# Second-layer matmuls of a fused attention and FFN block in 64-row halves, two units at a time

## The reference

```python
x = L0_attn_x                                    # 8 x 1024 x 256
q, k, v = split(x @ w_qkv.T + b_qkv)             # 16 heads of 16
q, k = rope(elu(q) + 1), rope(elu(k) + 1)
attn = softmax(q @ k.T / 4) @ v
x = layernorm(x + attn + conv3(v))
h = 2 * relu(s0 * concat(x, -x) @ sign(k0))      # 512 -> 1024
h = 2 * relu(s1 * h @ sign(k1))                  # 1024 -> 1024, the second layer
x = layernorm(x + s2 * h @ sign(k2))             # 1024 -> 256
```

## Time and profile before

| | |
|---|---|
| median of 3 runs | 2095.31 us (2095.06 to 2096.69) |
| profiled execution | 2094.53 us, its span 2092.4 us |
| TensorE busy | 2043.8 us, 98% of the span |
| VectorE busy | 1685.7 us, 81% |
| ScalarE busy | 1489.0 us, 71% |
| GpSimd busy | 1013.3 us, 48% |
| granted TensorE clock | 0.985 of full speed over the span |

### The profile page before, as it was taken

How to read it: one execution, slowest core, us unless ns; L and a number is a source line. 1 busy time by engine, 2 the same in 40 slices (tenths; PEclk the granted TensorE clock), 3 DMA queues, 4 the chain that set the end, 5 groups by cost and what they waited for, 6 DMA issues and landing times.

```text
span 2092.4 us, 43715 instructions
## 1 busy us (share of the span) xinstructions
PE 2043.8 (98%) x17150; PEld 802.9 (38%) x17150; DVE 1685.7 (81%) x3094; ACT 1489.0 (71%) x2867; POOL 1013.3 (48%) x583
## 2 busy tenths in 40 slices
PE   5999999999999999999999999999999999999998
PEld 3132323343433434334343343434343343434355
DVE  8989988788887988888887888878888788888143
ACT  3399888766877678776787767777687766867642
POOL 2968287614757158462585328661475704300010
PEclk7699999999999999999999999999999999999999
DMA  5001210020010200021000200002001010000000
GB/s 199 20 17 47 72 24 31 22 72 13 15 37 31 80 16 16 30 77 42 9 27 27 89 22 17 29 16 99 12 17 37 29 62 17 17 9 29 1 21 21
DMA packets 40429, 76.87 MB, mean 37 GB/s; under 512 B 15024, under 2 KB 19488, under 8 KB 37280
## 3 DMA queue, kind: packets, MB, share of 16 engines
q1 hardware_dynamic: 34496, 49.97, 8.3%
q0 software_dynamic: 5184, 23.07, 3.0%
q10 hardware_dynamic: 544, 1.05, 0.1%
HBM read 46.27 MB, written 25.17 MB: 34 GB/s over the span
## 4 chain that ended last, share of the span: by engine, by line
PE 86%; DVE 8%; ACT 3%; issue 1%; SPq 0%; DMA 0%; POOL 0%; POOLq 0%; ACTq 0%
PE unit_banks L761 27%; PE unit_banks L625 22%; PE o_bank L670 22%; PE unit_banks L697 5%; PE unit_banks L774 5%; DVE maxima L1032 5%; ACT probs L855 2%; PE unit_banks L685 2%; PE unit_banks L635 2%; DVE hT L1101 1%; PE unit_banks L678 1%; ACT rows L943 0%; DMA lepe_rows<-in_b_v 0%; ACT work L897 0%; DVE rows L1161 0%
## 5 line engine op out<-in xcount | busy, mean ns | idle before, releaser
L1032 DVE TENSOR_REDUCE maxima<-unit_banks 128x1 f32<-128x512 f32 x2048 | 1302.5, 682 | 285.4 <-PE unit_banks L625 281.7
L855 ACT ACTIVATE probs<-unit_banks 128x512 f32<-128x512 f32 x2048 | 1115.5, 605 | 491.1 <-PE unit_banks L635 487.6
L625 PE MATMUL unit_banks<-k_stack,q_stack 48*128 48x512 f16 x2048 | 636.5, 388 | 6.2 <-DVE maxima L1032 2.7
L635 PE MATMUL unit_banks<-q_stack,k_stack 50*128 50x512 f16 x2048 | 634.0, 383 | 5.3 <-ACT probs L855 3.2
L670 PE MATMUL o_bank<-probs,v_pair 128*32 128x256 f32 x8192 | 565.3, 387 | 4.0 <-issue 4.0
L761 PE MATMUL unit_banks<-h0T,w 128*128 128x512 f16 x2048 | 480.2, 380 | 0.1
L1439 POOL TENSOR_TENSOR attn<-o_rows_sb,rden 128x256 f32<-128x256 f32 x63 | 39.2, 622 | 743.1 <-DVE rden L1045 739.5
L670 PEld LDWEIGHTS o_bank<-probs,v_pair 128*32 128x32 f32 x8192 | 207.0, 109 | 306.3 <-issue 206.0
L625 PEld LDWEIGHTS unit_banks<-k_stack,q_stack 48*128 48x128 f16 x2048 | 121.8, 94 | 433.2 <-issue 241.3
L761 PEld LDWEIGHTS unit_banks<-h0T,w 128*128 128x128 f16 x2048 | 188.6, 98 | 249.3 <-issue 55.6
L1104 DVE SCALAR_TENSOR_TENSOR h1T<-unit_banks,h1T 128x512 f16<-128x512 f32 x128 | 87.3, 682 | 77.9 <-ACT h1T L919 77.8
(11 more groups left out here) (151 smaller groups left out, 1677.8 us busy)
## 6 DMA issues: line engine op xcount, KB each, us to landing
rows<-in_x POOLq DMA_DIRECT2D x8, 1024.0 KB, 6.3
q_stack<-q_scratch SPq DMA_DIRECT2D x128, 64.0 KB, 2.0
k_stack<-k_scratch SPq DMA_DIRECT2D x128, 64.0 KB, 2.0
work<-in_xT SPq DMA_DIRECT2D x7, 1024.0 KB, 8.1
q_scratch<-parts POOLq DMA_DIRECT2D x14, 512.0 KB, 3.3
k_scratch<-parts POOLq DMA_DIRECT2D x14, 512.0 KB, 3.2
out<-rows SPq DMA_DIRECT2D x7, 1024.0 KB, 4.9
q_stack<-q_scratch SPq DMA_DIRECT2D x128, 32.0 KB, 1.9
```

The source lines that it names most:

```text
L625: nc.tensor.matmul(units.out(unit), q_stack[row:row + STACK, r, t * P:(t + 1) * P], k_stack[row:row + STACK, r, half * 512:(half + 1) * 51 ...
L635: nc.tensor.matmul(units.out(unit), k_stack[row:end, r, kt * P:(kt + 1) * P], q_stack[row:end, r, half * 512:(half + 1) * 512], start=True ...
L855: nc.scalar.activation(probs[:, 2 * (kt % 2) + h, half * 512:(half + 1) * 512], units.out(unit), ACT.Exp, scale=exp_regs[2 * (n % PAIRS) + ...
L1032: nc.vector.reduce_max(maxima[:, v // T % 2, h * T + t, half:half + 1], units.out(unit), AXIS_X)\
```

## The change

Two neighbouring units of the second layer are made together, as a pair (`hidden_pair`). Each hidden tile of 128 rows is split into its upper and lower 64 rows. In the first half of the work (parts 0 and 1) the first unit takes the products over rows 0 to 63 and the second those over rows 64 to 127; in the second half (parts 2 and 3) they cross over. So two matmuls of 64 rows stand side by side at any time, each in its own bank, as S and T do. A pair has four pieces of 16 half matmuls where two units had four pieces of 8 whole ones. In front of part 2 TensorE waits for a new semaphore, that both units' first halves have ended. Both units end with part 3. All units of the second layer are in pairs but the last batch's and the last two units of the batch before it: 220 pieces are changed.

The steps of the pieces in the table are the same for most; the numbers are now written per piece (`deal_at`). A pair takes two banks with part 0 and gives both back after part 3. `Units` counts 0.9 for each of the two units of a piece, where it counted 1.4 for a piece.

```diff
+def in_pair(unit):
+    return unit[0] == "L1" and unit[1] < NB - 1 and not (unit[1:3] == (NB - 2, 1) and unit[3] >= KF - 2)
+
+def units_of(piece):
+    unit = piece[0]
+    return [unit, unit[:3] + (unit[3] + 1,)] if in_pair(unit) else [unit]
...
 def pieces_of(unit):
+    if in_pair(unit):
+        return [(unit, part) for part in range(4)] if unit[3] % 2 == 0 else []
...
         if m < TAIL - 1:
-            deal(b + 26, hidden_units("L1", m, 0, range(1)))
...
-            deal(b + 36, hidden_units("L1", m, 0, range(3, KF)))
+            deal_at(b, (26, 27, 29, 31, 33, *range(35, 46)), hidden_units("L1", m, 0))
             deal(b + 47, hidden_units("L0", m, 1), 2)
             deal(b + 54, out_units(m, 0))
-            deal(b + 58, hidden_units("L1", m, 1, range(6)))
...
+            deal_at(b, (*range(58, 70), 71, 73, 75, 77), hidden_units("L1", m, 1))
...
-DENSE_WRITING = 1.4
+DENSE_WRITING, SHARED_WRITING = 1.4, 0.9
...
+            crossings = [0]
+
+            def hidden_pair(first, second, part):
+                _, m, th, u = first
+                phase, quarter = divmod(part, 2)
+                if part == 0:
+                    units.wait_free(pe, first)
+                    units.wait_free(pe, second)
+                    crossings[0] += 2
+                elif part == 2:
+                    pe.wait_ge(rows_crossed, crossings[0])
+                for k in range(4 * quarter, 4 * quarter + 4):
+                    if u == 0 and phase == 0:
+                        units.wait_read(pe, ("L0", m, th, k))
+                    for i in range(2):
+                        for side in range(2):
+                            unit = second if side != phase else first
+                            r = slice(ROWS * side, ROWS * (side + 1))
+                            done = nc.tensor.matmul(units.out(unit), w1[r, k, unit[3] * P:(unit[3] + 1) * P], h0T[r, i, k, :],
+                                                    start=phase == 0 and k == 0 and i == 0,
+                                                    stop=phase == 1 and k == KF - 1 and i == 1, skip_group_check=True)
+                            if k == KF - 1 and i == 1:
+                                done.then_inc(units.full_sem(unit) if phase == 1 else rows_crossed, 1)
```

More of the change, by code:

```diff
@@ L140, in deal, with deal_at @@
             at[step + i // a_step].append(piece)
+    def deal_at(b, places, units):
+        for place, piece in zip(places, (piece for u in units for piece in pieces_of(u))):
+            at[b + place].append(piece)
     for c in range(1, NB):
@@ L159, in dealt @@
         if m < TAIL - 1:
-            deal(b + 26, hidden_units("L1", m, 0, range(1)))
-            for i, piece in enumerate(piece for u in hidden_units("L1", m, 0, range(1, 3)) for piece in pieces_of(u)):
-                at[b + 29 + 2 * i].append(piece)
-            deal(b + 36, hidden_units("L1", m, 0, range(3, KF)))
+            deal_at(b, (26, 27, 29, 31, 33, *range(35, 46)), hidden_units("L1", m, 0))
             deal(b + 47, hidden_units("L0", m, 1), 2)
             deal(b + 54, out_units(m, 0))
-            deal(b + 58, hidden_units("L1", m, 1, range(6)))
-            for i, piece in enumerate(piece for u in hidden_units("L1", m, 1, range(6, KF)) for piece in pieces_of(u)):
-                at[b + 71 + 2 * i].append(piece)
+            deal_at(b, (*range(58, 70), 71, 73, 75, 77), hidden_units("L1", m, 1))
             deal(b + 79, out_units(m, 1))
@@ L187, in done_within @@
 def done_within(s):
-    return [u for u, part in DEALT[s][:-1] if ends_unit((u, part))] if 0 <= s < STEPS else []
+    return [u for piece in DEALT[s][:-1] if ends_unit(piece) for u in units_of(piece)] if 0 <= s < STEPS else []
 def done_behind(s):
-    return [u for u, part in DEALT[s][-1:] if ends_unit((u, part))] if 0 <= s < STEPS else []
+    return [u for piece in DEALT[s][-1:] if ends_unit(piece) for u in units_of(piece)] if 0 <= s < STEPS else []
 def own_units(s):
@@ L237, in program_order @@
                     yield u, True, True, True
-                for u, part in DEALT.get(s, ()):
-                    ends = ends_unit((u, part))
-                    yield u, part == 0, ends, ends and u not in done_behind(s)
+                for piece in DEALT.get(s, ()):
+                    for u in units_of(piece):
+                        yield u, piece[1] == 0, ends_unit(piece), ends_unit(piece) and u not in done_behind(s)
             elif s > 0:
@@ L276, in __init__ @@
             if takes or ends or not read:
-                now += WRITING.get(u[0], DENSE_WRITING)
+                now += WRITING.get(u[0], SHARED_WRITING if in_pair(u) else DENSE_WRITING)
             if ends:
@@ L282, in __init__ @@
                 self.nth_full[u], self.nth_free[u] = full_count[first], free_count[last]
+                if in_pair(u) and u[3] % 2 == 1:
+                    self.nth_full[u[:3] + (u[3] - 1,)] = self.nth_full[u]
                 if u[0] in HIDDEN:
@@ L465, in build @@
         pv_done = sem("pv_done")
+        rows_crossed = sem("first_row_halves_done")
         o_copied = sem("o_copied")
@@ L792, in dense @@
                     ffn_out(unit, part)
+                elif in_pair(unit):
+                    hidden_pair(*units_of((unit, part)), part)
                 else:
```

## The result

The changed kernel took 2107.59 us (median of 4 runs, 2105.54 to 2109.03), the kernel before 2095.18 on the same chips (median of 4, 2093.55 to 2096.69). The ratio is 1.0059, with a 95% interval of 1.0041 to 1.0076: slower by 0.4 to 0.8%. Forecast were 2103 and slower, with a range from 2091 to 2119. The 12.4 us between the medians lie just above the band of 5 to 12 us that had a chance of 0.59.

A forecast was written before the change was run, and what follows sets the result against it. TensorE was taken to bound the kernel. Waits of 37.1 us less a gain of 29.8 gave +7.3 on the profiled 2094.5, so 2101.8; the median 0.8 above made 2102.6, said as 2103, range 2091 to 2119.

The forecast's parts named there:

- Gain: 142 pieces standing alone between bursts each lose two changes of form on TensorE, 0.21 us: -29.8 us.
- Slot: In changed pieces, two halves take a slot of 0.216 us, as one whole matmul did; 1760 slots, no added cost.
- second and third rivals: Second: slots of 0.226, 2121 us, chance 0.10. Third: loads unhidden, about 2268, or halves serial, about 2483; chance 0.04 together.
- TensorE goes on 0.06 later: At waits for a bank, TensorE resumes 0.06 us after the reader's read ends, taken from a matmul at the start.
- a: Steps 38 and 62, in batch 7 30 and 38: pair directly behind the burst waits 0.73 us, 14 places, +10.2.
- b: Steps 29 and 13: transpose of the maxima takes the burst's first S bank, waits 0.63 us, 11 places, +6.9.
- c: Behind a step's four transposes: 11 projections (steps 10 and 34) wait 0.14 us, 14 pairs wait 0.04, +2.1.
- d: Steps 42 and 2, and 34 of batch 7: pair waits for ScalarE's read of first T, 0.40 us, 13 places, +5.2.
- e: Behind steps 35 and 11, the next burst's last T waits for ScalarE, 0.38 us, 11 places, +4.2; without copy +0.8.
- f: Steps 7 and 33: pair waits for VectorE's read of the previous step's last S, 0.92 and 0.26 us, +6.2.
- g: Batch 7's steps with nothing dealt, three alone pieces without gain, and steps 13 to 15: estimated +1.5 us, ends 0 and 4.
- first rival: Waits on late readers (d, e, f, g: 17.9 us) vanish as ScalarE and VectorE catch up: 2085 us, chance 0.13.

The follow-up runs named there:

- experiment 3: Changed kernel with only pairs whose neighbours are whole units, their banks read long before they begin, 60 pieces: 2085.91 us, ratio 0.9953.
- experiment 4: Kernel before, with only the three second-layer pairs of the last batch's second half (its steps 50 to 61) made in halves: 2091.35 us, ratio 0.9977.
- experiment 6: Changed kernel with only the waits in front of pairs and the transpose of the maxima reordered, one covered wait left out: 2101.99 us, ratio 1.0034.
- experiment 1: Changed kernel with whole matmuls instead of halves; pairs keep their two banks and waits: 2137.15 us, ratio 1.02.
- experiment 2: Changed kernel with units 6 and 7 of the second half of batches 0 to 5 single again, 24 of 220 pieces: 2099.84 us, ratio 1.0015.
- experiment 7: Kernel of experiment 5 with the waits reordered as in experiment 6: 2081.25 us, ratio 0.9931.
- experiment 5: Changed kernel with only two spaced pairs a half where there is room, plus those of the last steps, 116 pieces: 2080.71 us, ratio 0.993.

## Why the prediction was right, point by point

Direction and range held; the size was 7.3 us where 12.4 were measured. Of the 13.5 us between the two profiled spans some 3 do not come of the waits, and most of them go with the clock that TensorE was granted. The rows of step 15 of batch 3 show it (length, busy time of the engines, granted clock as the third number from the end). Changed, the whole step and a stretch in it, then before:

```profile
809.35:815.45 6.10, 6.04 (x49) 3.36 (x46) 3.52 (x9) 3.55 (x9) 5.92 (x3) 0.72 0.12 28
811.00:812.00 1.00, 1.00 (x7) 0.69 (x6) 0.76 (x4) 0.82 (x2) 1.00 (x1) 0.50 0.01 2
802.04:807.00 4.96, 4.59 (x48) 2.65 (x45) 3.48 (x9) 4.03 (x10) 4.80 (x3) 1.00 0.24 61
```

From about 811 to 814 us TensorE ran at the lower of its two levels (0.50, 1.2 GHz), and the 16 matmuls of the third layer (L815, before L774) took 3.25 us there, 1.76 before: 1.6 us in this one step, which the same step of the other batches does not have. Just ahead, from 807 to 809, TensorE had been busy for 1.45 of 2.00 us. The start adds 2.5: 0.45 before the first step, which the clock does not explain (0.73 where it was 0.70), and 2.1 in batch 0, where no pair exists, with the clock at 0.56 in steps 2 and 3 where it was 0.82, and at 0.84 in steps 57 to 59 where it was 1.00. In steps 15 to 17 of batch 1 it is the other way round, 1.00 for 0.84, and 1.1 us come back. The trace of experiment 3 has the late start, the gain in batch 1 and a low step 15 (0.74, in batch 2) too, that of experiment 4 none of them; experiment 6 has all the pairs of the change, its low step 15 in batch 4, and 0.97 in steps 2 and 3. Whether pairs make such a stretch likelier is not shown: the traces of the change and of experiments 1, 2, 3, 6 and 7 have one low step 15 in batches 2 to 6, those of before, 4 and 5 have theirs in batch 1 alone. That leaves 10.5 to explain.

- **Gain.** Right: -0.21 per alone piece (-0.20 in steps 9, 11, 31 and 35), by the rows of step 39. That the halves are worth 29.6 us by experiment 1 and 29.8 were said is partly chance: in the last steps the prediction was wrong, eight of them gained 0.63 each, 3.4 us more than counted (experiment 4), and at the waits the halves gave less. The gain was said to be sure to about 1 us; it was not.
- **Slot.** Right at 0.216: 1.73 / 8. The bound of 0.226, and the second and third rivals with it, fell. A half's load is for rows on which an earlier half is still at work, and still the spacing is that of the columns. The rule of the Trainium skill ("TensorE: Matmul & The Clock Gate", Part 3, the mechanism), that loads overlap running matmuls only when the row group differs, would have made each slot longer; the trace speaks against it, as it did for whole rows. The same section also lets a load for "the background weight buffer" go ahead of running matmuls, which would allow what the trace shows.
- **New semaphore.** Said to cost nothing, and so it was: alone pieces with part 2 (steps 0, 4 and 60) gain the full 0.21.
- **"TensorE goes on 0.06 later".** This step failed. The moments at which the reads end were right. In step 38 it said T0 + 1.11, and the rows above have 648.48 - 647.36 = 1.12, with the burst's first matmul at 647.36. But the pair began 0.14 later, at T0 + 1.26, where 1.17 was said. The same in step 7 of batch 3, in the chain of the changed kernel:

```profile
777.68 1.20 DVE maxima L1075 x2
778.88 0.14 issue
779.02 1.90 PE unit_banks L801 x16
```

Here the burst starts at 777.59: the read ends at T0 + 1.29 (said: 1.30) and the pair starts at 1.43 (said: 1.36). In step 42 of batch 2 (burst at 663.64) it is ScalarE, with two high parts ahead of its reads as foreseen:

```profile
664.49 0.64 ACT probs L898
665.13 0.14 issue
665.26 1.88 PE unit_banks L801 x15
```

The read ends at T0 + 1.49 (said: 1.47), the pair starts at 1.62 (said: 1.53). The 0.06 was read from S matmuls behind one wait and used for places with two. Experiment 6 puts the late wait first, and the terms come to what was said:

| term | said | in the change | in experiment 6 | places |
|---|---|---|---|---|
| a, pair behind the burst | 0.73 | 0.83 | 0.74 | 14 |
| b, transpose of the maxima | 0.63 | 0.72 | 0.64 | 11 |
| c, projection | 0.14 | 0.15 | 0.16 | 11 |
| c, pair | 0.04 | 0.10 | 0.05 | 14 |
| d, steps 42 and 2 | 0.40 | 0.50 | 0.41 | 13 |
| e, steps 36 and 12 | 0.38 | 0.38 | 0.37 | 11 |
| f, step 7 | 0.92 | 0.99 | 0.90 | 5 |
| f, step 33 | 0.26 | 0.26 | 0.18 | 6 |

For alone pieces a wait is the step's difference plus 0.21. A fault of 0.09 in one delay, met at some 60 places, is the main miss. Against what was said the waits of the table are 1.4 (a), 1.0 (b), 0.9 (c), 1.3 (d) and 0.4 us (f) longer, with e 5.1 in all. 7.3 + 5.1 - 3.4 (last steps) = 9.0, and the 1.5 up to 10.5 lie in g (said: 1.5, with ends at 0 and 4; the traces have 2.9, 2.5 in batch 7 and 0.08 a batch in steps 14 and 15). That the sum came as near as it did is in part luck: waits too short by 6.5 us and a gain too small by 3.4 stand against each other in it. Term e, where T matmuls with one wait do the waiting, held to the hundredth.
- **Readers.** The first rival (late readers catch up) fell: d, e and f are there in full in each of batches 2 to 6. In steps 14 and 15 something of it shows: 0.57 is lost and 0.49 comes back.
- **What would show it.** The waits for VectorE and ScalarE were to be longer by over 30 us in total. The three new entries make 26.7, and over the whole list it is 26.8 (55.1 for 28.3), so this sign was not met, though the waits were longer than said. An entry counts idle time, which starts only when the matmuls before have ended; in step 38 it is 0.66, where 0.83 are lost.

## What to carry to other kernels

Working two outputs side by side pays for its changes of form, but it takes two banks at once, and a bank freed in the same burst is a wait on a reader that was harmless before. Count the free banks at each place where a pair begins, and pair only where the reads are already over: 60 well-placed pieces gained 9.3 us (2.5 of them in the last steps) where all 220 lost 12.4. Put the wait that is expected to be late first, and leave out a wait that another one covers: that was worth 5.6 us in the kernel with all 220 pieces, and nothing that the medians tell in that of experiment 5, which hardly waits. And look for stretches in which half of the array is idle anyway; 12 pieces there gained about 4 us by the medians.

## What the runs showed of the hardware that was not expected

- With two waits in front of a matmul, the late one second, TensorE started 0.144 to 0.148 us after the read's end; with one wait, or with the late one first, 0.054 to 0.059. Some 60 places made 5 us of it: without the start and the low clock the change's trace is 10.5 us longer than that of before, that of experiment 6 is 5.3.
- Two 64-row matmuls of different kinds and different operands run side by side: a half of the second layer beside a T matmul of 50 rows starts 0.01 us from it, and a step is 0.63 us shorter. That half stands behind both T matmuls of the burst in the program, and yet it starts (1939.60) ahead of the second of them (1939.81).
- Changing between 64-row halves of one kind and of another costs nothing: the first S behind 16 halves takes 0.21, as within the burst, where it took 0.32 behind whole matmuls.
